# Routing the fifth group of tokens ahead of the sixth group's graph output, in a fused graph-network, attention and expert kernel

## The reference

```
xn = layernorm(x)                                     # x: 3125 tokens x 256
x  = x + gnn(xn, src, dst) + linear_attention(xn)     # gnn: segment_sum over 53125 edges,
                                                      #   three small layers (64, 32, 256), relu, + xn
tokens = layernorm(x)
x  = x + moe(tokens)
# moe: logits = tokens @ router_w.T     (8 experts)
#      top 2 of softmax(logits), weights normalised to sum to 1
#      out = tokens + sum over the 2 experts of weight * (gelu(tokens @ w1[e] + b1[e]) @ w2[e] + b2[e])
```

## Time and profile before

| | |
|---|---|
| median of 3 runs | 441.68 us (440.45 to 442.03) |
| the profiled execution | 441.83 us, span from first to last instruction 440.1 us |
| busy in the span | PE 408.4 us (93%), DVE 321.4 (73%), ACT 265.2 (60%), POOL 206.2 (47%) |
| mean granted TensorE clock | 0.971 |

### The profile page before, as it was taken

How to read it: one execution, slowest core, us unless ns; L and a number is a source line. 1 busy time by engine, 2 the same in 40 slices (tenths; PEclk the granted TensorE clock), 3 DMA queues, 4 the chain that set the end, 5 groups by cost and what they waited for, 6 DMA issues and landing times.

```text
span 440.1 us, 9960 instructions
## 1 busy us (share of the span) xinstructions
PE 408.4 (93%) x3193; PEld 323.3 (73%) x3193; DVE 321.4 (73%) x878; ACT 265.2 (60%) x645; POOL 206.2 (47%) x242
## 2 busy tenths in 40 slices
PE   1989899997999999999999999788999999999985
PEld 0878687876777777777755657555999999899875
DVE  3587959958899999999727555666777776666662
ACT  1757565576787888888825614623777776444442
POOL 6054778258235554455400213572454454545454
PEclk9999999999999999999999988759999999999999
DMA  8938210007599999998996931124466556557660
GB/s 205 188 81 255 73 27 2 3 1 149 102 175 170 154 163 177 146 176 174 171 211 206 333 88 62 61 100 128 141 198 193 181 176 159 164 177 176 178 184 24
DMA packets 112258, 63.08 MB, mean 143 GB/s; under 512 B 88545, under 2 KB 102762, under 8 KB 112206
## 3 DMA queue, kind: packets, MB, share of 16 engines
q1 hardware_dynamic: 105022, 47.12, 50.8%
q0 software_dynamic: 6368, 14.47, 9.4%
q10 hardware_dynamic: 816, 0.85, 0.8%
HBM read 22.96 MB, written 21.44 MB: 101 GB/s over the span
## 4 chain that ended last, share of the span: by engine, by line
PE 60%; DVE 16%; issue 9%; DMA 7%; POOL 5%; ACT 2%; SPq 1%; DVEq 0%; POOLq 0%
PE bank L1665 10%; PE bank L1676 10%; PE bank L1416 5%; DVE region_a L975 5%; PE bank L1366 4%; PE bank L1428 4%; PE bank L1331 4%; PE bank L1459 4%; PE bank L1340 3%; PE bank L1654 3%; DMA region_a<-xs_next 2%; PE bank L1578 2%; PE bank L1347 2%; DMA out<-region_a 2%; PE bank L1564 1%
## 5 line engine op out<-in xcount | busy, mean ns | idle before, releaser
L720 ACT CAST region_a<-bank 128x500 bf16<-128x500 f32 (+1 forms) x119 | 72.4, 671 | 15.7 <-PE bank L1366 14.8
L1665 PE MATMUL bank<-region_a,region_c 128*128 128x128 f32 x496 | 65.7, 275 | 0.0
L1676 PE MATMUL bank<-region_c,region_a 128*128 128x256 f32 x248 | 63.7, 379 | 0.0
L1665 PEld LDWEIGHTS bank<-region_a,region_c 128*128 128x128 f32 x496 | 60.3, 191 | 0.3
L818 ACT ACTIVATE region_a<-bank,region_c 128x128 f32<-128x128 f32 x124 | 39.0, 366 | 32.5 <-PE bank L1665 32.5
L1127 DVE COPY region_c<-region_w 128x1026 f32 x62 | 43.2, 697 | 20.1 <-issue 18.6
L981 DVE TENSOR_TENSOR region_a<-iota,locs 128x3200 bf16<-128x3200 bf16 x25 | 54.5, 2182 | 0.0
L1366 PE MATMUL bank<-region_a 128*128 128x125 bf16 x625 | 53.0, 219 | 1.5 <-ACT region_a L720 1.4
L1366 PEld LDWEIGHTS bank<-region_a 128*128 128x128 bf16 x625 | 42.2, 101 | 13.5 <-ACT region_a L720 3.2
L655 POOL DMA_INDIRECT xs_next<-region_a x31 | 32.6, 1051 | 38.9 <-DVE region_a L1289 36.7
L642 POOL DMA_INDIRECT xs<-rows,slot_i x25 | 25.0, 999 | 53.9 <-ACT rows L764 38.3
(11 more groups left out here) (246 smaller groups left out, 789.9 us busy)
## 6 DMA issues: line engine op xcount, KB each, us to landing
region_a<-xs_next SPq DMA_DIRECT2D x31, 259.0 KB, 3.0
region_w<-in_w SPq DMA_DIRECT2D x4, 1024.0 KB, 9.8
region_a<-xs SPq DMA_DIRECT2D x31, 131.0 KB, 2.4
rows<-in_x SPq DMA_DIRECT2D x5, 560.0 KB
xs_next<-null SPq DMA_DIRECT2D x8, 259.0 KB, 4.3
xs_next<-null SPq DMA_DIRECT2D x1, 1554.0 KB, 10.9
xs<-null SPq DMA_DIRECT2D x8, 131.0 KB, 3.2
xs<-null SPq DMA_DIRECT2D x1, 786.0 KB, 7.5
```

Of the source, the lines that this page charges most:

```text
L720: nc.scalar.copy(to, count_bank(n)[:, 0:w * TP].rearrange("p (c t u) -> p c t u", c=w, t=NT)).then_inc(adj_done, 1)
L1665: last = nc.tensor.matmul(hid_ps[c % 2][:, f * P:(f + 1) * P], wc[:, c % 3, k * D + f * P:k * D + (f + 1) * P], xT[:, c % 2, k * P:(k + 1) ...
L1676: last = nc.tensor.matmul(y_ps[c % 2][:, 0:D], hT[:, c % 2, f * P:(f + 1) * P], wc[:, c % 3, (2 + f) * D:(3 + f) * D], start=False, stop=( ...
```

## The change

It takes the sixth group's `graph3`, `add_graph` and `scale` out of the places where they stood among the steps of groups 3 and 4, and puts them behind the fifth group's `choose`, `positions` and `weigh`. On DVE the order becomes: `scale(4)`, `choose(3)`, `weigh(3)`, `choose(4)`, `weigh(4)`, `add_graph(5)`, `sure_chunks`, `scale(5)`, `choose(5)`, `weigh(5)`. On PE `graph3(5)` moves behind `logits(4)`, and `transpose_tokens(5)` behind `positions(4)`. `logits(4)` loses its wait for the sixth group's `x2_done`, and the extra tile of `graph3(5)` waits for the fifth group's logits to be read. The instructions themselves, their shapes and their number stay.

```diff
@@ VectorE
-            for g in range(NR):
-                if g + 1 < NR:
-                    scale(g + 1)
+            for g in range(NR - 3):
+                scale(g + 1)
                 choose(g)
-                if g + 2 < NR:
-                    add_graph(g + 2)
+                add_graph(g + 2)
                 weigh(g)
-                if g == NR - 2:
-                    sure_chunks()
+            scale(NR - 2)
+            choose(NR - 3)
+            weigh(NR - 3)
+            choose(NR - 2)
+            weigh(NR - 2)
+            add_graph(NR - 1)
+            sure_chunks()
+            scale(NR - 1)
+            choose(NR - 1)
+            weigh(NR - 1)
@@ TensorE, graph3
-                        pe.wait_ge(lg_read, g - 1)
+                        pe.wait_ge(lg_read, g if g == NR - 1 else g - 1)
@@ TensorE, logits
-                if g + 1 < NR:
-                    pe.wait_ge(x2_done, ROUT[g + 1][1])
+                if g != NR - 2:
+                    pe.wait_ge(x2_done, ROUT[min(g + 1, NR - 1)][1])
@@ TensorE, order
-            for g in range(2, NR):
-                if g + 1 < NR:
-                    transpose_tokens(g + 1, 0)
-                if g + 2 < NR:
-                    graph3(g + 2)
-                positions(g)
-                if g + 1 < NR:
-                    keep_clock(spare, 3)
-                    logits(g + 1)
+            transpose_tokens(3, 0)
+            graph3(4)
+            positions(2)
+            keep_clock(spare, 3)
+            logits(3)
+            transpose_tokens(4, 0)
+            positions(3)
+            keep_clock(spare, 3)
+            logits(4)
+            graph3(5)
+            positions(4)
+            transpose_tokens(5, 0)
+            keep_clock(spare, 3)
+            logits(5)
+            positions(5)
```

## The result

The changed kernel takes 448.14 us (median of 4 runs, 445.85 to 449.37), the kernel before 441.86 (440.45 to 442.11): 1.0139 times as long, 95% interval 1.0107 to 1.0171. It is slower, by 6.3 us. The profiled execution took 448.74 us with a span of 447.0. All medians in this document are of runs in the chip's faster state, which leaves out one run of 452.65 us among the six of one experiment.

A forecast was written before the change was run, and what follows sets the result against it. Three chains (fifth group's scatter and sure rows, PE's queue, DVE's table) reach the experts within a few us; the sixth group's slots, 8.2 us later, delay chunk 3 by 7.6: 441.83 + 7.6 = 449.4, so 449.3 us (446.6 to 451.2).

The forecast's parts named there:

- What sets the start: Ahead of the expert chunks: the table and chunk 3's load give +7.6 us, PE's queue +7.2; the later one counts.
- The fifth group's logits and slots: On PE and DVE: `logits(4)` starts 0.9 us earlier, 1.3 if the fillers run fast; slots 0.9 earlier.
- The sixth group's chain: From `add_graph(5)` to `weigh(5)` over DVE, ACT and PE: the slots come 8.2 us later, although no step gets longer.
- The table: On DVE behind `weigh(5)`: 8.08 us to its end at 311.0; SP issues chunk 3's load 0.74 behind it.
- The load of chunk 3: SP's load behind the table: 2.63 us from issue to landing, so the rows land at 314.4, +7.6 us.
- The sum: Whole kernel: 441.83 + 7.6 = 449.4, median 0.15 lower, so 449.3 us; chance 0.70 for 448.3 to 450.4.
- The sure chunks start earlier: Rival at POOL: the fourth and fifth group's transfers come up to 1.66 us earlier, giving 440.2 us; chance 0.03.
- The sure chunks cover it: Rival on PE: three chunks fill 6.3 us of the delay while the sixth group is routed, no change; chance 0.03.
- The clock: PE's clock taken as low for the sixth group; rival: full clock there, 1.8 us less, 447.5 us; chance 0.13.
- The clock low longer: Rival on PE: all 26 `keep_clock` products take 11.1 us instead of 7.99, 452.0 us; slow `logits(4)`, 451.4; chance 0.07.
- A smaller delay: Rival: gaps close up between steps, 0.3 us at each of eight hand-overs, 2.4 in all, 446.9 us; chance 0.04.

## Why the prediction was right

It said 449.3 us, between 446.6 and 451.2; 448.14 was measured. Point by point, on the mark's clock:

- **What sets the start.** Right: the table and the load of chunk 3 end last, PE's queue 0.55 us ahead of them. Without the 14 products `turn_rows(3)` did not move. The delay alone, in the old order, gives the loss.
- **The fifth group's logits and slots.** 0.9 us earlier was forecast, 1.2 were measured, near the bound of 1.3 for fast fillers: the three ran in 0.65 us and not in 1.0.
- **The sixth group's chain.** 8.2 us later was forecast, 7.7 measured: the 0.3 of the point above, and 0.2 at the hand-overs. `add_graph(5)` 2.34 us, `sure_chunks` 2.8, the slow `logits(5)` 2.60 came as priced.
- **The table.** 8.02 us instead of 8.08, and SP's issue 0.74 behind it, as read.
- **The load of chunk 3.** This term was mis-sized by 0.5 us: 2.10 from issue to landing, not 2.63. The row that it was taken from is a load behind POOL's last scatters; at 310 us it is alone (DMA share 0.00 from 308 to 311 us). That the other traffic makes the difference was not tried by itself. The estimate of 2.3 us by the Trainium skill (DMA: Bandwidth & Descriptors, "Anatomy of one DMA") was nearer than the row.
- **The sum.** 7.6 less 0.3, 0.2 and 0.5 is 6.6, and 41.36 - 34.87 = 6.5 was measured at `turn_rows(3)`. From there to the end it took 133.3 us before and 134.1 after. In the other kernels it was 132.0 to 134.0, and 135.9 without the 14 products; the waits for rows in the second half of the chunks differ from one execution to the next (0.53 and 1.18 us before; 0.97, 0.80 and 0.81 after), which makes the 0.8 of this pair. It is not put down to the change.
- **The rivals.** *The sure chunks start earlier:* the rows were 2.3 us earlier, more than the 1.66 that was priced, and nobody took them; holding them back by 6.2 us cost nothing. *The sure chunks cover it:* they could not, their place in PE's queue is behind `positions(5)`. *The clock:* low, as taken, in the changed kernel; lifting it gave 1.8 us at the sixth group's slots, as forecast, and 1.6 at `turn_rows(3)`. *The clock low longer:* no, the 26 products took 7.27 us and not 11.1. *A smaller delay:* the hand-overs gave 0.2 us and not 2.4.

## What to carry to other kernels

When a chain of waits shows one way to the bound, look for the others that end within a microsecond or two of it: a step made earlier on the one is worth at most that much, and if it is made earlier at the cost of a step on another, the whole lateness counts. Before an order is changed, each step that moves back has to be checked for what it stood *under*: `add_graph(5)` cost nothing while DVE was waiting anyway, and the same 2.3 us and its followers made 6 us where nothing covered them. An edit's worth also depends on which way ends last at that moment: a shorter queue on PE gave nothing at `turn_rows(3)` in one order, and let the clock fall behind it, and it gave 1.0 us at the same place in another.

## What was not expected of the hardware

In a wait of 3.09 us on PE, in the midst of products at full clock, the granted clock fell from 1.00 to 0.50, and the next two chunks lost 2.8 us, where the products that had filled the wait cost nothing. Products on zeros put into the earlier gap did lift the clock for `logits(5)` (1.48 us instead of 2.60), but it was down again at 0.50 from 298 to 302 us, after `logits(5)` and a wait of 1.82 us, so the 26 clock-keeping products became no shorter: with a break of 0.22 us between them they ran from 299.00 to 307.2. Where a copy of 128x1026 words on DVE overlapped one of POOL's transfers, one of the two took longer: the copy 0.93 us instead of 0.70 (at 291.15 in the changed kernel), or POOL's instruction 1.27 and 1.35 us instead of 0.97 beside copies of 0.70 (at 290.14 and 295.53 before the change). This was not tried by itself. The Trainium skill (SBUF — State Buffer, "SBUF: two separate sides") states that a float copy of this kind on VectorE and GpSimd's writing of descriptors lock each other out of a shared port; the rows agree with that and show no more.
